# Second attention of a two-layer decoder: the top-64 mask applied as a penalty on GpSimd, softmax sums taken by ACT's exponential, one reciprocal for two tiles

## The reference, cut to what matters

```
q, k, v = split_heads(x @ Wq), ...            # 16 heads of 64
k, v = concatenate(memory of 16, k), ...      # 528 keys
dots = einsum('bhid,bhjd->bhij', q, k) * scale
dots = einsum('bhij,hk->bkij', dots, pre_proj)        # heads mixed
dots = where(causal, neg, dots)
vk = top_k(dots, 64)[0][..., -1:]
dots = where(dots < vk, neg, dots)                    # only the 64 largest stay
attn = softmax(dots)
attn = einsum('bhij,hk->bkij', attn, post_proj)       # heads mixed again
out = einsum('bhij,bhjd->bhid', attn, v)
return out @ Wo + bo
```

## Time and profile before

| | us |
|---|---|
| median of three runs | 4336.03 |
| the profiled execution | 4341.53 |
| its span | 4339.7 |
| DVE busy in the span | 2651.0 |
| PE busy in the span | 3051.6 |
| ACT busy in the span | 1075.5 |
| POOL busy in the span | 479.8 |

### The profile page before, as it was taken

One profiled execution on the slowest core, in us unless ns is written; L12 is line 12 of the kernel. 1 busy time (PEld: TensorE's weight loads), 2 busy tenths in 40 slices (PEclk: granted clock), 3 DMA queues, 4 the chain that ended last, 5 costly groups with the idle time before them and its releaser, 6 DMA issues. The chain is left out here.

```text
span 4339.7 us, 40948 instructions
## 1 busy us (share of the span) xinstructions
PE 3051.6 (70%) x12160; PEld 1873.7 (43%) x12160; DVE 2651.0 (61%) x8650; ACT 1075.5 (25%) x2485; POOL 479.8 (11%) x748
## 2 busy tenths in 40 slices
PE   5746964996575766677667755442697945999997
PEld 2324643765343453444445434321233632555554
DVE  5984654551389989998999899748433141111112
ACT  1114631440233333333333332110001110111111
POOL 3540002002010111111011111000220000000000
PEclk6558977997667877777777767665798956999998
DMA  2000014553221111111212111000100003000000
GB/s 77 0 0 18 1 68 135 165 169 101 69 82 57 55 64 60 58 54 58 73 41 71 49 57 30 4 29 0 52 0 20 0 4 97 1 0 0 0 0 19
DMA packets 158960, 199.62 MB, mean 46 GB/s; under 512 B 30750, under 2 KB 133731, under 8 KB 158758
## 3 DMA queue, kind: packets, MB, share of 16 engines
q1 hardware_dynamic: 155686, 188.85, 13.8%
q0 software_dynamic: 3072, 8.39, 0.6%
HBM read 136.12 MB, written 61.08 MB: 45 GB/s over the span
## 5 line engine op out<-in xcount | busy, mean ns | idle before, releaser
L1983 DVE MAX8 a_best<-a_rest 128x8 f32<-128x72 f32 (+28 forms) x1624 | 682.9, 465 | 0.0
L1721 PE MATMUL a_pmix<-a_rows,a_kpre 128*128 128x264 f32 (+41 forms) x528 | 271.3, 631 | 517.7 <-ACT a_mixed L1839 513.0
L1978 DVE MATCH_REPLACE8 a_rest<-a_best,a_rest 128x72 f32<-128x72 f32 (+28 forms) x1392 | 626.8, 461 | 0.0
L2765 DVE TENSOR_TENSOR e_hT<-e_act_out,e_pc 128x512 f32<-128x512 f32 x128 | 88.1, 688 | 481.2 <-ACT e_act_out L2756 424.4
L1721 PEld LDWEIGHTS a_pmix<-a_rows,a_kpre 128*128 128x128 f32 x528 | 118.5, 273 | 603.8 <-issue 598.1
L1730 PEld LDWEIGHTS a_pat<-a_kp,a_probs 128*128 128x128 f32 x1344 | 265.6, 286 | 76.8 <-issue 37.1
L1730 PE MATMUL a_pat<-a_kp,a_probs 128*128 128x128 f32 x1344 | 265.6, 371 | 38.4 <-POOL a_kp L1947 34.7
L1947 POOL TENSOR_SCALAR a_kp<-a_kpost,a_rden 128x128 f32<-128x128 f32 x256 | 151.9, 605 | 1233.6 <-DVE a_rden L1995 1233.6
L2719 PE MATMUL e_ph<-xT,e_w 128*128 x512 | 247.2, 606 | 55.0 <-PEq L2682 46.0
L2736 PE MATMUL e_py<-e_w,e_hT 128*128 128x256 f32 x1024 | 254.4, 391 | 0.0
L1711 PE MATMUL a_psc<-a_kT,branch 64*128 64x264 f32 (+3 forms) x640 | 188.7, 497 | 30.3 <-ACT a_stage L1808 28.6
(11 more groups left out here) (442 smaller groups left out, 5385.2 us busy)
## 6 DMA issues: line engine op xcount, KB each, us to landing
f_w<-in_L_ffn_W SPq DMA_DIRECT2D x39, 1024.0 KB, 5.8
l_scores<-a_stage SPq DMA_DIRECT2D x32, 528.0 KB, 2.7
l_scores<-a_stage SPq DMA_DIRECT2D x32, 400.0 KB, 2.5
l_scores<-a_stage SPq DMA_DIRECT2D x32, 272.0 KB, 2.1
f0o_w<-in_L_ffn_W SPq DMA_DIRECT2D x8, 1024.0 KB, 12.6
sorted_x<-z_blank SPq DMA_DIRECT2D x1, 4992.0 KB, 17.2
f_xs<-sorted_x SPq DMA_DIRECT2D x39, 128.0 KB, 5.4
sorted_y<-f_ys SPq DMA_DIRECT2D x39, 128.0 KB, 5.7
```

What stands on the lines that cost most here:

```text
L1721: ins = pe.matmul(pmix[:, at, 0:hi - lo], kpre[:], rows[:, g % 4, lo:hi], start=True, stop=True)
L1978: last[a] = signal(dve.match_replace(rest[:, a, 0:wd], best[:, a, q - 1, :], rows_of[a] if q == 1 else rest[:, a, 0:wd], GONE))
L1983: last[a] = signal(dve.max(best[:, a, q, :], rest[:, a, 0:wd]))
```

## The change

For searched tiles the exponential no longer runs beside the search. When the floor is found, POOL writes a penalty into `probs` (-1e30 where the score is below the floor, else 0) and then the score plus the penalty into `probs`; ACT takes the exponential of that in place, and has the sum written by the same instruction (`accum_out`). For tiles that are not searched ACT takes it from `mixed` as before, now with the sum. DVE's masked multiplication is gone. Its reciprocals are taken for both tiles of a pair in one instruction (`invert`), for pair k-1 behind the fourth of the seven rounds of pair k, or behind the two MAX8 where pair k is not searched. POOL's weighting of `kp` for k-1 stands behind the edge of k+1. `mixed` is free once the masked row is written. ACT in step k now does the exponentials of k-1, then `mixed_out` of k+1 and the negated maximum of k, then the fills of `side(k)`, `post_out` of k-1, and then output and heads (`products`). PE in step k does `mix`, the fills of `side(k)`, `post` of k-1, then `products`.

```
--- before.py
+++ after.py
@@ -1542,10 +1542,11 @@
...
         mix_full, mixed_ready, cut_done, top_ready = sem("mix_full"), sem("mixed_ready"), sem("cut_done"), sem("top_ready")
-        neg_ready, exp_ready, sums_ready, kp_ready = sem("neg_ready"), sem("exp_ready"), sem("sums_ready"), sem("kp_ready")
+        neg_ready, sums_ready, kp_ready = sem("neg_ready"), sem("sums_ready"), sem("kp_ready")
...
             sem("zeroed"), sem("post_full"), sem("aT_ready"), sem("o_full"), sem("o_read"))
-        dve_steps = sem("dve_steps")
+        dve_steps, found, compared, masked, inverted = (
+            sem("dve_steps"), sem("found"), sem("compared"), sem("masked"), sem("inverted"))
@@ -1568,6 +1569,14 @@
...
             return max((x + 1 for x in range(max(g - 3, 0), g) if banks(x) & banks(g)), default=0)
+        def searched(g):
+            return l1_tile(g)[3] > TOP1
+        def searches(g):
+            return sum(searched(x) for x in range(g))
@@ -1772,6 +1781,8 @@
...
                             project(kind, x, j)
+                def products(k):
@@ -1791,11 +1802,13 @@
...
                             mix(2 * (k + 2) + a)
+                    if k >= 0:
+                        side(k)
...
                     if k >= 0:
-                        side(k)
+                        products(k)
@@ -1832,24 +1845,32 @@
...
                     act.wait_ge(mix_full, g + 1)
-                    if g >= 4:
+                    if g >= 4 and searched(g - 4):
+                        act.wait_ge(masked, searches(g - 3))
+                    elif g >= 4:
...
+                def negated(g):
+                    act.wait_ge(top_ready, g + 1)
+                    act.activation(negmax[:, g % 4:g % 4 + 1], best[:, g % 2, 0, 0:1], ACT.Identity, scale=-scale
+                                   ).then_inc(neg_ready, 1)
...
                     n, i, r, wd = l1_tile(g)
-                    m = negmax[:, g % 4:g % 4 + 1]
-                    act.wait_ge(top_ready, g + 1)
-                    act.activation(m, best[:, g % 2, 0, 0:1], ACT.Identity, scale=-scale).then_inc(neg_ready, 1)
+                    x = mixed[:, g % 4, 0:wd]
+                    if searched(g):
+                        act.wait_ge(masked, searches(g + 1))
+                        x = probs[:, g % 4, 0:wd]
...
                     act.wait_ge(neg_ready, g + 1)
-                    act.activation(probs[:, g % 4, 0:wd], mixed[:, g % 4, 0:wd], ACT.Exp, bias=m, scale=scale
-                                   ).then_inc(exp_ready, 1)
+                    act.activation(probs[:, g % 4, 0:wd], x, ACT.Exp, bias=negmax[:, g % 4:g % 4 + 1], scale=scale,
+                                   accum_out=den[:, g % 4:g % 4 + 1]).then_inc(sums_ready, 1)
@@ -1897,15 +1920,20 @@
...
                     for a in range(2):
+                        if k >= 1:
+                            exps(2 * (k - 1) + a)
+                    for a in range(2):
...
                         if 0 <= k < PAIRS1:
-                            exps(2 * k + a)
+                            negated(2 * k + a)
+                    if k >= 0:
+                        side(k)
...
                     if k >= 0:
-                        side(k)
+                        products(k)
@@ -1917,15 +1945,17 @@
...
                 pool.wait_ge(loaded, LOADS)
+                def weights(k):
+                    for a in range(2):
+                        g = 2 * k + a
+                        pool.wait_ge(inverted, k + 1)
+                        if g >= 4:
+                            pool.wait_ge(post_full, g - 3)
+                        pool.tensor_scalar(kp[:, g % 4, :], kpost[:], rden[:, g % 4:g % 4 + 1], None, ALU.mult
+                                           ).then_inc(kp_ready, 1)
...
                     n, s = k // STEPS1, k % STEPS1
-                    if k >= 0 and s < 2:
-                        i = l1_group(n)[1]
-                        for a in range(2):
-                            g = 2 * k + a
-                            if g >= 4:
-                                pool.wait_ge(post_full, g - 3)
-                            pool.memset(probs[:, g % 4, i * P:(i + 2) * P], 0.0).then_inc(zeroed, 1)
@@ -1938,14 +1968,33 @@
...
                             pool.tensor_tensor(x, x, cut[:], ALU.add).then_inc(cut_done, 1)
+                        g = 2 * k + a
+                        if k >= 0 and s < 2:
+                            if g >= 4:
+                                pool.wait_ge(post_full, g - 3)
+                            i = l1_group(n)[1]
+                            pool.memset(probs[:, g % 4, i * P:(i + 2) * P], 0.0).then_inc(zeroed, 1)
+                    if k >= 1:
+                        weights(k - 1)
...
                         g = 2 * k + a
-                        if k >= 0:
-                            pool.wait_ge(sums_ready, g + 1)
+                        if k >= 0 and searched(g):
+                            wd = l1_tile(g)[3]
+                            p, x = probs[:, g % 4, 0:wd], mixed[:, g % 4, 0:wd]
...
                                 pool.wait_ge(post_full, g - 3)
-                            pool.tensor_scalar(kp[:, g % 4, :], kpost[:], rden[:, g % 4:g % 4 + 1], None, ALU.mult
-                                               ).then_inc(kp_ready, 1)
+                            pool.wait_ge(zeroed, 4 * n + min(2 * s + a + 1, 4))
+                            pool.wait_ge(found, searches(g + 1))
+                            pool.tensor_scalar(p, x, best[:, a, TOP1 // 8 - 1, 7:8], HIDE, ALU.is_lt, ALU.mult
+                                               ).then_inc(compared, 1)
+                    for a in range(2):
+                        g = 2 * k + a
+                        if k >= 0 and searched(g):
+                            wd = l1_tile(g)[3]
+                            p, x = probs[:, g % 4, 0:wd], mixed[:, g % 4, 0:wd]
+                            pool.wait_ge(compared, searches(g + 1))
+                            pool.tensor_tensor(p, x, p, ALU.add).then_inc(masked, 1)
+                weights(PAIRS1 - 1)
@@ -1959,40 +2008,47 @@
...
                     dve.wait_ge(dve_steps, step)
+                def invert(k):
+                    x = slice(2 * k % 4, 2 * k % 4 + 2)
+                    dve.wait_ge(sums_ready, 2 * k + 2)
+                    if k >= 2:
+                        dve.wait_ge(kp_ready, 2 * (k - 1))
+                    dve.reciprocal(rden[:, x], den[:, x]).then_inc(inverted, 1)
...
                     rows_of = [mixed[:, g % 4, 0:wd] for _, g, wd in lanes]
-                    floor = [GONE, GONE]
...
                         dve.wait_ge(cut_done, g + 1)
+                        if g >= 2:
+                            dve.wait_ge(neg_ready, g - 1)
                         dve.max(best[:, a, 0, :], rows_of[a]).then_inc(top_ready, 1)
-                    if lanes[0][2] > TOP1:
-                        for q in range(1, TOP1 // 8):
-                            for a, g, wd in lanes:
-                                if q == 1:
-                                    dve.wait_ge(top_ready, g + 1)
-                                else:
-                                    after(last[a])
-                                last[a] = signal(dve.match_replace(
-                                    rest[:, a, 0:wd], best[:, a, q - 1, :], rows_of[a] if q == 1 else rest[:, a, 0:wd],
-                                    GONE))
-                            for a, g, wd in lanes:
+                    if lanes[0][2] <= TOP1:
+                        if pair >= 1:
+                            invert(pair - 1)
+                        continue
+                    for q in range(1, TOP1 // 8):
+                        for a, g, wd in lanes:
+                            if q == 1:
+                                dve.wait_ge(top_ready, g + 1)
+                            else:
                                 after(last[a])
+                            last[a] = signal(dve.match_replace(
+                                rest[:, a, 0:wd], best[:, a, q - 1, :], rows_of[a] if q == 1 else rest[:, a, 0:wd],
+                                GONE))
+                        for a, g, wd in lanes:
+                            after(last[a])
+                            if q < TOP1 // 8 - 1:
                                 last[a] = signal(dve.max(best[:, a, q, :], rest[:, a, 0:wd]))
-                        floor = [best[:, a, TOP1 // 8 - 1, 7:8] for a in range(2)]
-                    for a, g, wd in lanes:
-                        dve.wait_ge(exp_ready, g + 1)
-                        if g >= 4:
-                            dve.wait_ge(kp_ready, g - 3)
-                        after(last[a])
-                        p = probs[:, g % 4, 0:wd]
-                        last[a] = signal(dve.scalar_tensor_tensor(p, rows_of[a], floor[a], p, ALU.is_ge, ALU.mult,
-                                                                  accum_out=den[:, g % 4:g % 4 + 1]))
```

(10 more changed lines are left out.)

## The result

Faster by 1.5%: 4267.7 us (median of 4 runs, 4265.08 to 4271.33) against 4337.2 (4 runs on the same chip, 4331.67 to 4339.83), ratio 0.985 with a 95% interval of 0.983 to 0.986. The forecast was 4284. The medians differ by 69.5 us, where 52 were forecast. The profiled execution took 4270.31 us with a span of 4268.5.

A forecast was written before the change was run, and what follows sets the result against it. DVE was taken to bound the second attention, busy 1542.71 of 1613.00 us. 129 us removed, less 17, 32, 20, 3.6 and 4.8, gave 52 us: 4284 for the median, forecast range 4267 to 4326 (chance 0.59).

The forecast's parts named there:

- (a): Group changes cost a third to a half of the sum, as PE interleaves `post` better; about 4255 us, chance 0.20.
- removed from DVE: Masked multiplications, accumulator reads and two reciprocals ending each of 116 searched pairs: mean 1.115 us, 129 us in all.
- reciprocal for two: DVE gets back one reciprocal over two columns per pair: 0.15 us each, 17 us, ends 12 and 35.
- wide to narrow: 520/528 followed by 152/160: 8.7 us of waits in three batches, 5.5 in the last; 32 us, ends 24 and 57.
- behind a batch: From 392/400 through 24/32 to the first searched pair: 22.0 us for 15.4, three times; 20 us, ends 16 and 34.
- first pairs: At the start the first two searched pairs bring nothing (2.3 us) and the order costs some 1.3: 3.6 us.
- The mask's chain: From search's end: two comparisons, two additions, second exponential, then the reciprocal; 7.4 us at 520, against 11.5 of cover.
- C: GpSimd's comparison per searched tile: 0.19 us + 3.2 ns a column, 1.86 us at 520 and 1.47 at 400.
- A: GpSimd's addition per searched tile: 0.19 us + 2.1 ns a column, 1.28 us at 520 and 1.03 at 400.
- (c): Comparison costs 9.5 ns a column on GpSimd, deciding from about 8: slower, 4407 us, chance 0.08.
- (b): PE's chain becomes late in ordinary narrow pairs, 1.4 us in nine per batch, 50 us: 4334, no change; chance 0.10.
- (d): GpSimd locks DVE's searches out, 4 us in each of 116 pairs: 460 us, about 4745; chance 0.03.

The follow-up runs named there:

- a_q1: The changed kernel with the query projections one step later, so the narrow pair behind a wide one has none: 4260.02 us, ratio 0.983.
- a_now: The changed kernel with the exponentials of unsearched pairs taken in their own step, as before the change: 4261.79 us, ratio 0.983.
- a_sidelate: The changed kernel with `side` behind `post` and `post_out` again, as before the change: 4298.4 us, ratio 0.991.
- a_cmp2: The changed kernel with the comparison on GpSimd done twice: 4310.63 us, ratio 1.0006.
- a_three: The changed kernel with query projections later, unsearched pairs' exponentials in their own step, and DVE comparing in eight last pairs of wide groups: 4234.25 us.
- b_recip1: The kernel before, with only one reciprocal over two columns in place of two: 4314.97 us, ratio 1.0016.

## Why the prediction was right

The mechanism was the one forecast, and the sum was 13.5 us too cautious. Predicted 51.6 (129 less 77.4); measured by the lengths of the pairs, before and after, 65.1, as below (in us). The medians moved by some 4 us more than the stage, for which no term stands here and nothing was changed. The two large misses, 7 and 10 us, go the same way: 4267.7 lies at the very edge of the forecast's own range (4267 to 4326), and nearer to rival (a)'s 4255 than to 4284. That it was the forecast and not (a) is told by the lengths of the pairs alone, not by the time.

```
term                               predicted   measured
removed from DVE                        129      127.8
reciprocal for two                      -17       -9.9
wide to narrow, 4 times                 -32      -22.1
behind a batch, 3 times                 -20      -18.7
first pairs                            -3.6       -5.4
last pair                              -4.8       -4.8
waits that I had not seen                 0       -1.8
sum                                      52         65
```

- **What is removed.** Summed over all searched pairs of the trace of before, first multiplication to next MAX8 (or, for the last one, to the end of its reciprocal) is 129.2 us; the last pair's 1.38 was already in the last term, a small double count.
- **The reciprocal**, taken at 0.15 a pair, is the first mis-sized term. The widest pairs became 1.50 us shorter with 1.58 removed, so 0.08 each; what the eye takes for its price, the 154 ns of its row, overlaps the instruction behind it. The same difference has a median of 0.07 over the 105 ordinary pairs, 8.5 us for 116. The 9.9 of the table is no measurement of its own: it is what is left of the sum, small waits included.
- **The mask's chain.** C was taken at 1.86 us and measured 2.03 at 520 columns (1.47 and 1.62 at 400); A at 1.28, measured 1.279; the chain at 7.4, measured 7.36. That the last is so near is luck in part: the two comparisons take 0.34 us more than predicted, and the chain starts 0.32 before the next pair's MAX8 (1382.54 and 1382.86 above), which the prediction did not count. The nearest row, the weighting, was the right one, within a tenth. Of what would have made C slow nothing is seen: 541 ns at 72 columns and 2034 at 520 are 3.3 ns a column. The rule that I set beside rival (c), some 10 ns an element where code branches on data (the Trainium skill, GPSIMD Engine Reference, "Performance versus the Vector engine"), does not bear on this comparison: 3.3 was measured, not 10.
- **Wide to narrow** is the second mis-sized term. The first stall was put at 3.0 and measured 2.73. The second was put at 5.7 and measured 3.94, 3.83 and 3.34. In the last batch, which has no projections, both were put at 5.5 together; by the prediction's own steps it is 8.7 less the 4.4 of the projections, 4.3, and 2.8 were measured. I had carried `post` over with its durations of before, 2.34 and 2.47 us. Those ran at a granted clock of 0.50, 1.2 GHz:

```profile
1398.80:1404.60 5.80, 4.87 (x22) 4.60 (x22) 5.80 (x35) 0.75 (x2) 0.39 (x1) 0.50 0.07 20
```

That is the kernel before, columns as in the earlier trace rows. With the projections ahead of it, `post` follows on 5.1 us of unbroken matmuls and runs at 1.00, 2.4 GHz, in 1.28 and 1.35. Part of this is given back by the projections, which now come first and take 5.29 us in place of 4.37. So the products account for 2.18 - 0.92 = 1.3 of the 1.8 us; most of the rest is the two exponentials at the end of this chain, put at 1.2 us and done in 0.8. That the projections ahead are what raises the clock is shown for the first tile only: it took 1.28 us behind them in three batches, and 2.50 without them in a_q1 and in the last batch here. The second tile ran at the higher clock without them too, in the last batch (granted clock 1.00) and in three of the four of a_q1, and at 0.50 in the first batch of a_q1; why, these runs do not show:

```profile
2539.82 2.50 PE L1739 MATMUL a_pat<-a_kp,a_probs 128*128 128x128 f32 x10
2543.25 1.35 PE L1739 MATMUL a_pat<-a_kp,a_probs 128*128 128x128 f32 x10 [0.94 <-ACT a_edge L1886]
```
- **Behind a batch**: predicted 22.0 us a time, measured 20.85, 22.78 and 22.26 against 15.37, 15.91 and 15.93.
- **First pairs**: 47.35 against 44.04 for the first five, and 2.1 not saved. a_now gives 3 of it back, so it is the order of the exponentials.
- **Not seen**: the values' projections of the second batch make one wide pair wait 1.5 us.
- **Rivals.** (a), the group changes costing a third to a half of my sum: they cost 51 of the 60 us summed, so it fell. (b): the narrow pairs do not wait, but for the two behind a wide one; the five searched ones behind a batch's end take 31.0 to 31.3 us where they took 34.3 to 34.6. a_sidelate does not bring it either: its new waits, up to 5.25 us, stand in the first steps of the wide groups, which no rival named. In the changed kernel only the new order keeps these away. (c): a_cmp2 puts its edge near where the prediction did, but the loss there is larger, 73 us for 52. (d): refuted, MAX8 696 to 698 ns beside GpSimd and 692 without. The port rule that I named (the Trainium skill, SBUF - State Buffer, "SBUF: two separate sides") lets a DVE operation with one SBUF input pass outside the two-port modes, and by that the trace agrees.

## What to carry to other kernels

Time taken from a saturated engine counts in full, and work given to an idle one is free as long as its chain fits under the next unit of work: price the chain, not the engine, and do it where the next unit is shorter and where there is none. There the opposite division can be right: here the comparison belongs on GpSimd in 108 pairs and on DVE in 8, and these 8 bring 26 us. Before moving a waiting instruction or the work ahead of it, ask what starts at it and what the new place stands in front of: of four such moves the two that took work out of a late chain paid (10 and 7 us), and the two that put it elsewhere in the same chain did not.

## What the runs showed of the hardware

- GpSimd's tensor_scalar with two operations and a scalar for each row takes about 0.30 us + 3.3 ns a column (541 ns at 72, 1623 at 400, 2034 at 520). At 128 columns it takes 717 ns, and the weighting, with one operation, 605: the second operation costs about a fifth more, not the same again. DVE does the same comparison in 460 ns at a mean of 460 columns (a_three), where GpSimd takes about 1.8 us.
- A small DVE instruction far from its producer costs the queue about half of what its record says (0.08 against 0.154 us); right behind its producer, the idle time of 0.10 before it comes on top (b_recip1).
- The same ten matmuls took 2.34 to 2.50 us at a granted clock of 0.50 and 1.28 to 1.35 at 1.00. Putting 5.1 us of PE's own unbroken products ahead of them brought the first ten to 1.00 in all three batches where it was done (1.28 us), and without them they took 2.50; the next ten were found at either clock in one and the same kernel (a_q1: 2.47 us in the first batch, 1.35 in the others).
